# Where the bias of a graph layer's hops is added: a selector product on TensorE, or a second VectorE operation

## The reference, cut to what matters

```
H = 0;  Xk = X
for k in range(3):
    H = H + Xk @ Wk[k] + bk[k]
    Xk = transition @ Xk            # transition: 512 x 512 for each graph, rows normalised
return relu(H)                      # the caller adds it to x
```

## Time and profile before

| | |
|---|---|
| median of 3 runs | 1603.48 us |
| the profiled execution | 1603.98 us, of which the span of the trace is 1602.0 us |
| granted TensorE clock, mean | 0.983 of full speed |
| VectorE busy | 1192.0 us (74%), 2667 instructions |
| ScalarE busy | 886.4 us (55%) |
| GpSimd busy | 285.6 us (18%) |
| DMA | 92.21 MB, 17.4% of the 16 engines' span |

### The profile page before, as it was taken

The page is one execution under the profiler, slowest core; times in us unless marked ns, Lnnn a source line. Parts: engine busy times, 40 slices in busy tenths (PEclk is TensorE's granted clock), DMA queues, the critical chain, the costliest instruction groups (busy, mean ns, idle before and its releaser), DMA issues.

```text
span 1602.0 us, 28213 instructions
## 1 busy us (share of the span) xinstructions
PE 1476.8 (92%) x10426; PEld 1117.6 (70%) x10426; DVE 1192.0 (74%) x2667; ACT 886.4 (55%) x1501; POOL 285.6 (18%) x348
## 2 busy tenths in 40 slices
PE   5778799999999999999999999999999999999985
PEld 4677677768777677777767777776777777677733
DVE  6465877978778777777878777787777778787673
ACT  3334455564565656556565655656465565656564
POOL 3211021213012030211203021130311103030001
PEclk9789999999999999999999999999999999999998
DMA  7010112002210302121020212102121211021021
GB/s 228 1 53 14 61 47 80 27 27 73 66 60 14 109 30 65 59 79 59 13 95 32 76 59 79 59 13 74 50 79 59 66 72 52 27 85 41 14 68 38
DMA packets 58554, 92.21 MB, mean 58 GB/s; under 512 B 4289, under 2 KB 23297, under 8 KB 58497
## 3 DMA queue, kind: packets, MB, share of 16 engines
q1 hardware_dynamic: 58496, 91.44, 17.4%
HBM read 83.04 MB, written 8.39 MB: 57 GB/s over the span
## 4 chain that ended last, share of the span: by engine, by line
PE 65%; issue 16%; DVE 10%; ACT 5%; POOL 2%; DMA 1%; ACTq 0%; POOLq 0%; SPq 0%; DVEq 0%
PE ring_f L1360 41%; PE ring_b L1360 9%; PE ring_b L1640 6%; PE pv_acc L1656 6%; PE ring_f L1537 2%; POOL rstd L501 2%; ACT hf L580 1%; DVE att L1191 1%; DVE m L992 1%; ACT uz L570 1%; DVE bns L951 1%; DVE tr_l L992 1%; DVE uz L992 1%; PE ring_f L1437 1%; DVE rows L1119 1%
## 5 line engine op out<-in xcount | busy, mean ns | idle before, releaser
L1191 DVE TENSOR_TENSOR att<-ring_b,at 128x1024 f32<-128x1024 f32 x256 | 308.2, 1219 | 93.5 <-PE ring_b L1640 89.0
L728 ACT ACTIVATE att<-att 128x1024 f32<-128x1024 f32 x256 | 268.3, 1055 | 163.8 <-DVE att L1191 162.5
L501 POOL TENSOR_TENSOR rstd<-var,mhalf 128x4 f32<-128x4 f32 x80 | 81.7, 1021 | 735.4 <-DVE var L966 735.3
L1360 PE MATMUL ring_f<-w,uz 128*128 128x256 f32 (+1 forms) x896 | 197.0, 342 | 2.4 <-DVE uz L992 1.8
L1360 PE MATMUL ring_f<-m,tr_h 128*128 128x256 f32 x1024 | 190.8, 287 | 0.0
L1360 PEld LDWEIGHTS ring_f<-w,uz 128*128 128x128 f32 x896 | 150.7, 191 | 34.7 <-DVE uz L992 7.5
L1360 PEld LDWEIGHTS ring_f<-m,tr_h 128*128 128x128 f32 x1024 | 158.6, 191 | 22.8 <-issue 22.0
L1360 PEld LDWEIGHTS ring_f<-m,inc_n 128*128 128x128 f32 x1024 | 129.2, 197 | 37.0 <-issue 26.6
L1360 PE MATMUL ring_f<-m,inc_n 128*128 128x256 f32 x1024 | 136.3, 291 | 16.3 <-POOL m L505 16.2
L1360 PE MATMUL ring_f<-m,tr_l 128*128 128x256 f32 x512 | 144.5, 282 | 0.0
L1656 PE MATMUL pv_acc<-att,xp_n 128*32 128x512 f32 x1024 | 134.9, 604 | 4.6 <-ACT att L728 3.5
(11 more groups left out here) (178 smaller groups left out, 2787.1 us busy)
## 6 DMA issues: line engine op xcount, KB each, us to landing
at<-in_adjT SPq DMA_DIRECT2D x32, 1024.0 KB, 6.8
rows<-in_adjT SPq DMA_DIRECT2D x16, 1024.0 KB, 6.1
adj_n<-in_adj SPq DMA_DIRECT2D x16, 1024.0 KB, 5.2
x_in<-in_x SPq DMA_DIRECT2D x16, 512.0 KB, 3.9
out_x<-h SPq DMA_DIRECT2D x16, 512.0 KB, 6.9
wrow<-in_adj SPq DMA_DIRECT2D x16, 256.0 KB, 5.5
att<-in_Wk SPq DMA_DIRECT2D x3, 256.0 KB, 5.5
att<-in_W1T SPq DMA_DIRECT2D x1, 512.0 KB, 9.3
```

What stands on the lines that cost most here:

```text
L501: pool.tensor_tensor(rstd[k][:], var[k][:], mhalf[:], ALU.pow).then_inc(rstd_made[k].sem, 1)
L728: act.activation(v, v, ACT.Tanh).then_inc(tanh_made.sem, 1)
L1191: dve.tensor_tensor(att[:, u % 2, 2 * half:2 * half + 2], ring_b[half][:], at[:, u % NT].unsqueeze(1).broadcast_to([P, 2, N]), ALU.mult).t ...
L1360: ins = pe.matmul(dst, lhsT, rhs, start=(first and n == 0), stop=(last and n == len(pairs) - 1), skip_group_check=True)
```

## The change

The bias is no longer part of TensorE's sum. It lies in `bk_bc`, the sum of the three rows on all 128 partitions, and VectorE adds it while it takes X2 out of PSUM. That makes two operations for each bank in place of one: xa = X2 + bk_bc, and, behind a wait for that operation, xa = max(xa, 0) + xf. The first reads PSUM and SBUF, the second two SBUF tiles. The selector products and the tiles `sel` and `rowb` go, with their set-up: four memsets, two copies and a subtraction. The two sums of the bias rows and the three loads run over 128 partitions and no longer over 64. The places of the steps in the lists stay.

```diff
-                    (xh_t[0:64, 0, 0:256], bk[0:1, :].broadcast_to([64, D])),
-                    (xh_t[0:64, 0, 256:512], bk[1:2, :].broadcast_to([64, D])),
+                    (xh_t[:, 0, 0:256], bk[0:1, :].broadcast_to([P, D])),
+                    (xh_t[:, 0, 256:512], bk[1:2, :].broadcast_to([P, D])),
                 ):
                     sp.dma_start(dst, src).then_inc(par_loaded, 16)
-                sp.dma_start(xh_t[0:64, 1, 0:256], bk[2:3, :].broadcast_to([64, D])).then_inc(par_loaded, 16)
+                sp.dma_start(xh_t[:, 1, 0:256], bk[2:3, :].broadcast_to([P, D])).then_inc(par_loaded, 16)
...
             def set_up_w2():
-                step(dve.memset(sel[:].bitcast(F32), 0.0))
-                step(dve.memset(rowb[:].bitcast(F32), 0.0), now=True)
-                step(dve.memset(sel[0:1].bitcast(F32), 1.0))
-                step(dve.memset(sel[32:33].bitcast(F32), 1.0))
...
             def set_up_rest():
-                step(dve.tensor_tensor(xh_t[0:64, 0, 0:D], xh_t[0:64, 0, 0:D], xh_t[0:64, 0, D:2 * D], ALU.add), now=True)
-                step(dve.tensor_tensor(xh_t[0:64, 0, 0:D], xh_t[0:64, 0, 0:D], xh_t[0:64, 1, 0:D], ALU.add), now=True)
-                bias_row(xh_t[0:64, 0, 0:D], xc_s[0:64, 0, 0:D])
+                step(dve.tensor_tensor(bk_bc[:], xh_t[:, 0, 0:D], xh_t[:, 0, D:2 * D], ALU.add), now=True)
+                step(dve.tensor_tensor(bk_bc[:], bk_bc[:], xh_t[:, 1, 0:D], ALU.add), now=True)
...
                 dve.wait_ge(x2_full.sem, x2_full.after(g, k + 1))
-                dve.scalar_tensor_tensor(xa[:, v], bank_of(X2, k)[:].rearrange("p (t d) -> p t d", t=2), 0.0,
-                                         xf[:, v], ALU.max, ALU.add).then_inc(x2_out.sem, 1)
+                if k == 0:
+                    c_x2.begin()
+                c_x2.link(dve.tensor_tensor(xa[:, v], bank_of(X2, k)[:].rearrange("p (t d) -> p t d", t=2),
+                                            bk_bc[:].unsqueeze(1).broadcast_to([P, 2, D]), ALU.add))
+                here(c_x2, g)
+                dve.scalar_tensor_tensor(xa[:, v], xa[:, v], 0.0, xf[:, v], ALU.max, ALU.add).then_inc(x2_out.sem, 1)
...
-                        pairs = [(sel[:], rowb[:])] if bias else []
+                        pairs = []
```

More of the change, by code:

```diff
@@ L135, in graph_layers @@
         ct = sb("ct", [P, DT, P])
-        sel = sb("sel", [P, P], F32R)
-        rowb = sb("rowb", [P, D], F32R)
         rowz = sb("rowz", [P, D], F32R)
@@ L143, in graph_layers @@
         b2_bc = sb("b2_bc", [P, D])
+        bk_bc = sb("bk_bc", [P, D])
         v2_c = sb("v2_c", [P, DT, 2])
@@ L267, in graph_layers @@
         c_rs = Chain(sem("c_rs"), 3)
+        c_x2 = Chain(sem("c_x2"), 2)
         c_stat = Chain(sem("c_stat"), 2)
@@ L342, in graph_layers @@
         W1_LOADS, PARAM_LOADS, MORE_LOADS = 3, 11, 6
-        SET_W1, SET_COLUMNS, SET_W2, SET_DONE = 1, 12, 24, 42
+        SET_W1, SET_COLUMNS, SET_W2, SET_DONE = 1, 12, 20, 35
         stage, stage2 = att[:].rearrange("p a h n -> p (a h n)"), hb[:].rearrange("p t d -> p (t d)")
@@ L872, in split @@
                 step(dve.tensor_tensor(dst_lo, src, dst_hi.bitcast(F32), ALU.subtract))
[L874 to L877, removed]
             def set_up_w1():
@@ L1538, in f_tt, with hop_own @@
                 ins.then_inc(tt_full.sem, 1)
-            def hop_own(g, name, w_at, bias):
+            def hop_own(g, name, w_at):
                 pe.wait_ge(h1_lo.sem, h1_lo.after(g, 2))
@@ L1564, in f_r1 @@
             def f_r1(g):
-                hop_own(g, R, D, False)
+                hop_own(g, R, D)
             def f_r(g, part):
@@ L1573, in f_x1 @@
             def f_x1(g):
-                hop_own(g, X2, 0, True)
+                hop_own(g, X2, 0)
             def f_x2(g, part):
```

## The result

The changed kernel takes 1607.93 us (median of 9 runs, 1605.68 to 1609.50) where the kernel before took 1603.48 (9 runs, 1602.44 to 1606.78). The ratio is 1.0023, its interval 1.0014 to 1.0031: slower, by 4.5 us, near the forecast of 1607. A second set of runs gave 1606.66 against 1604.51, ratio 1.0013 (1.0004 to 1.0022), so slower by 2.2 us. Both intervals lie above 1; between them they allow a loss of 0.6 to 5 us. The profiled execution took 1609.50 us, its span is 1607.5.

The account below looks back on a forecast made before the run. TensorE, busy 92% of the span, was taken to set the time. Terms 0.0 + 0.7 + 1.0 + 0.5 + 1.2 - 0.5 + 0.5 = +3.4 us on 1603.48 gave 1607 us, own range 1604 to 1610.

Parts of the forecast that it names:

- What TensorE saves: In f_x1, four selector products of 0.118 us fewer a graph: 0.47 us, over 16 graphs 7.5 us.
- What VectorE pays: In f_x2, a second operation waiting for the first: 0.72 us more a bank, 1.44 a graph, 23.0 in all.
- The round: In the loop, TensorE waits 0.6 us for f_u's low part; net of 0.47, +0.12 to +0.14 a round, +1.2 for ten.
- The other turns: Written-out turns, net: graph 0 0.0, graph 1 +0.7, graph 2 +1.0, graph 3 +0.5, graph 14 -0.5, graph 15 +0.5 us.
- Graph 14: Written-out turn: second f_x2 waited 0.68 us, the rest goes in a TensorE wait behind f_m's first half; net -0.5 us.
- Graph 15: Last turn: delay 1.31, idle time 0.25 ahead of the unit product, so 1.0 us late to the end; net +0.5.
- Rival 1: The cover behind f_x2 holds and all of TensorE's saving arrives: 1603.5 - 7.5 = 1596.0 us; chance 0.16.
- Rival 2: Saving and delay cancel: a bank at 0.60, not 0.72, takes 3 us off; time stays at 1603.5 us; chance 0.16.
- Rival 3: GpSimd meets the new second operation, 1.24 us in place of 0.69; 5.5 us over ten rounds, 1612.4 us; chance 0.14.

Follow-up runs that it names:

- the first experiment: The kernel before without its four selector products a graph, VectorE untouched, hops' bias left out of the result: 1598.99 us against 1604.51, ratio 0.9966.
- the second: The changed kernel with four selector products a graph put back on TensorE, with a selector of zeros: 1614.98 us against 1604.51, ratio 1.0071.
- the change again: The changed kernel, unedited, run and traced a second time: 1606.66 us against 1604.51 for the kernel before, ratio 1.0013.
- the seventh experiment: The change made in graphs 4 to 14 only, graphs 0 to 3 and 15 as in the kernel before: 1604.00 us against 1604.14, ratio 0.9999.
- the sixth experiment: Against the kernel before, in all turns: no selector products, one VectorE operation a bank, the additions on GpSimd: 1605.91 us against 1604.46, ratio 1.0006.
- the two spread kernels: The changed kernel with both additions before both maxima, bank freed early: all turns 1604.15 us (ratio 1.0000), graphs 4 to 14 only 1602.11 us (0.9987).
- the version for the loop alone: Additions on GpSimd in graphs 4 to 14 only, others as in the kernel before, bank freed by VectorE's operation: 1600.15 us against 1603.93, ratio 0.9981.
- the one for all turns: Additions on GpSimd in every turn, one VectorE operation a bank, no selector products: 1605.91 us against 1604.46 for the kernel before, ratio 1.0006.

## Why the prediction was right

**What TensorE saves** was near: 0.47 us a graph were worked out, and 0.40 to 0.43 arrive in the trace after and in the first experiment, 0.47 by the second. (A seventh of 0.82 is 0.117 and not 0.118; nothing hangs on it.)

**What VectorE pays** was right: 0.73 us a bank where 0.72 was taken; the wait of an operation for the one before it costs 0.03 us.

**The round** was right in its mechanism, with one term too large: the idle time ahead of `f_u` is gone, and TensorE waits ahead of `f_u` (0.13, predicted 0.12) and ahead of `f_conv1`. The size of the second was off: `f_u` came 876.87 - 873.15 - 2.99 = 0.73 us later against TensorE, where 0.85 was worked out, so that TensorE's stall is 0.47 in all and not 0.6. Net +0.04 us (0.47 lost, 0.43 gained) and not +0.12 to +0.14; over ten rounds 0.4 to 0.7 us, not 1.2. Of the 0.12 us the overlap of neighbours explains most: the prediction let `f_u` start at the end of the statistics, but an operation that follows another without idle time starts ahead of that one's end, here at 876.87 with the end at 876.21 + 0.74 = 876.95.

**The other turns**, from one graph's `f_stat` to the next, the change against before:

| graph | predicted | measured | remark |
|---|---|---|---|
| 0 | 0.0 | +0.3 | first trace; -2.1 in the change again, and -2.2 in the seventh experiment, which leaves this turn as before: the half-clock stretches differ |
| 1 | +0.7 | +0.75 | the change again; it and before have nearly the same stretches here; +0.34 in the first trace, where they differ |
| 2 | +1.0 | +1.2 | first trace, same stretches; `f_u` and, not foreseen, the scores wait; -0.4 in the change again, which lacks one stretch |
| 3 | +0.5 | +0.3 to +0.4 | both traces |
| 4 to 13 | +1.2 | +0.4 to +0.7 | both traces |
| 14 | -0.5 | 0.0 | missed: the bank of X2 0 |
| 15 | +0.5 | +1.6 to +1.8 | wait 1.0 longer as predicted, then half clock; +1.2 up to the last scores, the rest in the 16 products at the end |

These rows sum to +4.6 to +5.2, against +3.4. The medians say 2.2 and 4.5. The rows of graphs 1 and 2 are those of the trace whose half-clock stretches match before's, and the other trace gives less; so the rows of graphs 0 to 2 are good to a microsecond at best. Two steps failed. Graph 14: I followed VectorE's results to `f_m`, but not the bank that `f_m` 1 is written into, which waits for the second operation; the saving went there. Graph 15: the delay of 1.0 us and the net of +0.5 were right up to the scores (the shift goes from 3.69 to 3.25 with the selectors, and to 4.22 with the wait), but a stretch at half clock follows, which costs 0.5 us at once and 0.2 in the attend; another 0.4 to 0.5 us, in the 16 products at the end, may belong to the execution. The errors in the loop (-0.5 to -0.8), at 14 (+0.5) and at 15 (+1.1 to +1.3) went opposite ways. That the total lands within 1 us of the forecast is luck in that part; the way of the change and the mechanism in the loop are not.

**Rival 1** (the cover holds) fell: the cover is 0.83 us and the delay 1.46 at `f_m`; and with the whole saving arriving, the round would have been 93.7. **Rival 2** (the two cancel) is what happened in the loop, though not in the whole: a net too small to read. **Rival 3** (GpSimd and the new operation meet) did not occur in the loop: the second operation takes 0.69 there. The condition held where it was said to: at graph 2 one of the two took 0.81 beside a GpSimd step. And as the sixth experiment shows, it is dear where it does occur.

Where `f_dn` and GpSimd's operation meet, one of the two is held, the other keeps its length, and the starts in the trace do not tell which: GpSimd's stands 0.03 to 0.06 us ahead in every such round, and was yet the one held in three rounds of ten of the kernel before and of each of the two spread kernels.
The Trainium skill (SBUF — State Buffer, section Who interferes with whom) calls the shared ports an exclusive lock and lets the order of issue decide who is blocked. The runs agree with the lock; whether the order of issue decides, they cannot show, and the order of the starts in the trace does not.

## What to carry to other kernels

Work taken off the busiest engine can be lost again at a wait for the engine that got the work. Take, for each wait behind the edit, the cover (idle time of both engines) from the delay, and set what is left against the saving; here 0.47 us stood against 0.43, and the two cancelled. Follow the storage too: a step that delays the release of a bank delays whoever writes that bank next, and the release should hang on the last read, not on the last result. And put such a change only into the turns that have the cover; here, with the bank freed early, the version for the loop alone gained 3.8 us where the one for all turns gained nothing.

## What was not expected of the hardware

- The clock after a wait. In the last turn TensorE stands 0.87 us, then 1.52. In the five traces (of four kernels) whose last turn has this longer wait (1.39 to 1.53 us), the scores behind it ran at half clock, 1.45 to 1.65 us in place of 0.97. In the seven with 0.54 or 0.69 us at this place they ran at full clock. These seven have a wait of 1.40 to 1.68 us ahead of the next scores: all seven ran those at full clock too, and two fell to half in the transposes behind them. So the length of a wait alone does not decide. That the two waits in a row are the cause is argued from this, not tested by itself.
- Executions of one kernel differ in where half-clock stretches lie during the first 260 us, which makes a microsecond or two in the length of those turns; a comparison of turns there needs the clock beside it.
- A VectorE operation on 128x4, 0.16 us long, took 1.23 beside a GpSimd operation on 128x512, and GpSimd's own took 1.73 where it takes 1.28 alone.
- Which of VectorE and GpSimd is held changes from round to round of one execution, and in a chain without cover the round is 0.2 us longer or shorter by it.
